# A two-layer transformer on one core: attention begins in another order, sums of x and y are spread, second bank for the slots' outputs, other order of gathers, fewer sort products

## The reference, cut to what matters

```python
x = x + L0_xattn(ctx_1024, layernorm(x))   # state-space scan over 256 steps, gated by silu(z); z = layernorm(x)
x = x + L0_ffn(layernorm(x))               # 32 experts of width 96, all computed, 8 of them weighted
x = x + L1_xattn(layernorm(x), ctx_1024)   # q = x @ Wq, 16 heads, 8 kv heads, softmax, @ Wo
x = x + L1_ffn(layernorm(x))               # shared part + top 2 of 16 experts

# L1_ffn
shared = swiglu(x, wg_s, wu_s, wd_s) * 0.1
affinity = sigmoid(einsum('bsh,eh->bse', x, centroids))
_, top_idx = top_k(affinity + gate_bias, 2)
weights = top_aff / (top_aff.sum(-1, keepdims=True) + 1e-9)
for e in range(16):
    routed = routed + mask[..., e:e + 1] * swiglu(x, wg[e], wu[e], wd[e])
return shared + routed
```

## Time and profile before

| | us |
|---|---|
| median of 3 runs | 692.14 (691.43 to 693.7) |
| the profiled execution, its own time | 690.36 |
| its span | 688.6 |
| TensorE busy | 625.7 (91%) |
| VectorE busy | 488.7 (71%) |
| ScalarE busy | 385.8 (56%) |
| GpSimd busy | 275.2 (40%) |

### The profile page before, as it was taken

How to read it: one execution, slowest core, us unless ns; L and a number is a source line. 1 busy time by engine, 2 the same in 40 slices (tenths; PEclk the granted TensorE clock), 3 DMA queues, 4 the chain that set the end, 5 groups by cost and what they waited for, 6 DMA issues and landing times.

```text
span 688.6 us, 10769 instructions
## 1 busy us (share of the span) xinstructions
PE 625.7 (91%) x3640; PEld 511.1 (74%) x3640; DVE 488.7 (71%) x1034; ACT 385.8 (56%) x790; POOL 275.2 (40%) x280
## 2 busy tenths in 40 slices
PE   7657759999999999999979999999999999999894
PEld 2346535554677888888868999999899988778773
DVE  5999999999976565446456766668577865654365
ACT  4866667644146546445367777777876765423221
POOL 1356610002144444445444655655455861241204
PEclk9789999999999999999999999999999999999998
DMA  6677844665645354444229232242111221355524
GB/s 194 200 270 265 278 156 149 204 204 178 182 130 173 104 177 124 154 153 150 79 90 339 96 135 79 83 147 78 32 31 47 78 78 47 123 171 166 181 96 122
DMA packets 58134, 98.89 MB, mean 144 GB/s; under 512 B 7000, under 2 KB 26976, under 8 KB 58080
## 3 DMA queue, kind: packets, MB, share of 16 engines
q1 hardware_dynamic: 56544, 94.00, 43.0%
q0 software_dynamic: 1536, 4.20, 1.9%
HBM read 78.51 MB, written 19.66 MB: 143 GB/s over the span
## 4 chain that ended last, share of the span: by engine, by line
PE 58%; DVE 26%; issue 7%; ACT 6%; another core or an unknown queue 1%; POOL 1%; DMA 0%; DVEq 0%; SPq 0%; ACTq 0%; POOLq 0%
PE bank L97 15%; PE bank L98 14%; PE bank L99 14%; DVE state L1432 10%; PE bank L884 5%; DVE read_out L1442 4%; PE bank L822 3%; PE bank L905 2%; ACT probs L1262 2%; PE bank L873 2%; ACT bank L1015 1%; DVE u_sb L1358 1%; DVE x_tok L1456 1%; DVE bank L1697 1%
## 5 line engine op out<-in xcount | busy, mean ns | idle before, releaser
L1994 POOL TENSOR_TENSOR w_lo<-w_raw,w_hi 128x768 fp32r<-128x768 f32 (+1 forms) x70 | 112.5, 1609 | 171.7 <-ACT w_hi L979 169.4
L97 PE MATMUL bank<-xt_hi,w_hi 128*128 128x512 f32 x224 | 91.1, 406 | 1.3 <-DVE hidden_lo L1349 1.3
L98 PE MATMUL bank<-xt_lo,w_hi 128*128 128x512 f32 x224 | 88.7, 396 | 0.0
L99 PE MATMUL bank<-xt_hi,w_lo 128*128 128x512 f32 x224 | 88.5, 395 | 0.0
L979 ACT ACTIVATE w_hi<-w_raw 128x768 fp32r<-128x768 f32 (+1 forms) x70 | 52.1, 745 | 58.4 <-PE bank L99 46.4
L1262 ACT ACTIVATE probs<-scores,row_min 128x256 f32<-128x256 f32 x128 | 63.8, 501 | 18.7 <-DVE row_min L1825 18.5
L2101 POOL TENSOR_TENSOR probs<-probs,row_scale 128x512 f32<-128x512 f32 x64 | 66.6, 1040 | 5.0
L1825 DVE CUSTOM_DVE_ANT_0 scores<-bank,mask_bias 128x256 f32<-128x256 f32 x128 | 48.8, 419 | 18.7 <-PE bank L99 18.7
L979 ACT ACTIVATE probs_t_hi<-bank 128x512 fp32r<-128x512 f32 x64 | 38.2, 598 | 36.8 <-PE bank L822 36.1
L510 PEld LDWEIGHTS bank<-identity,read_out 128*128 128x128 f32 x272 | 34.4, 153 | 30.8 <-DVE read_out L1442 17.9
L1130 ACT ACTIVATE gated<-bank 128x512 f32<-128x512 f32 x52 | 31.1, 597 | 42.1 <-PE bank L604 26.9
(11 more groups left out here) (233 smaller groups left out, 1747.0 us busy)
## 6 DMA issues: line engine op xcount, KB each, us to landing
w_raw<-in_ffn_w SPq DMA_DIRECT2D x38, 384.0 KB, 3.5
b_rows<-bc_scratch SPq DMA_DIRECT2D x32, 256.0 KB, 4.9
c_rows<-bc_scratch SPq DMA_DIRECT2D x32, 256.0 KB, 4.0
w_raw<-fold_scratch SPq DMA_DIRECT2D x32, 256.0 KB, 2.9
experts<-in_ffn_w SPq DMA_DIRECT2D x16, 384.0 KB, 4.2
route_bc<-route_scratch SPq DMA_DIRECT2D x31, 192.0 KB, 3.4
slots_scratch<-nothing SPq DMA_DIRECT2D x2, 2944.0 KB, 13.2
slots_in<-slots_scratch SPq DMA_DIRECT2D x22, 256.0 KB
```

What stands on the lines that cost most here:

```text
L97: e.matmul(out, w_hi, m_hi, start=first, stop=False)
L98: e.matmul(out, w_hi, m_lo, start=False, stop=False)
L99: return e.matmul(out, w_lo, m_hi, start=False, stop=last)
L1994: e.tensor_tensor(lo[:, 0:n], w_raw[(p - WHOLE) % RAW][:, 0:n], hi[:, 0:n].bitcast(F32), ALU.subtract).then_inc(sem("w_lo"), 1)
```

## The change

Six edits, none of which adds or drops a result:

1. y's sums of the second half: the first batch's stay where they were, the second batch's and the variance move to the next FFN unit.
2. Attention's beginning. `project(0, 0)` stands before `down(U0 - 1)`; `scores(0)` and `scores(1)` come next, and only then `project(0, 1)` and `project(1, 0)`. ACT and DVE follow that order. The table of exponentials is loaded after the FFN's last silu. Weight pieces are split one unit later.
3. The steps of x for the second half move from units 2 to 7 to units 3 (both additions), 5 and 7 (sums), 9 (variance), 10 (POOL's power), 11 and 12 (normalising), 13 and 15 (transposes and their splits).
4. `sel_sums` holds running sums of `sel` over the chunks, made by DVE with a copy and three additions; `count_earlier` needs 3 products in place of 8.
5. `down_slots` uses bank 3 for the odd rounds 9 to 21, bank 2 for all others.
6. The lower slots (m = 1) are gathered and added first, and their gathers wait for all rounds of the half but the last; the higher slots' gathers wait for that one too.

```diff
+        def out_bank(r):
+            return 3 if r % 2 == 1 and 9 <= r <= ROUNDS - 2 else 2
...
-                for j in range(1, HC):
-                    e.matmul(ps[:, j * E1:HC * E1], every[:, :], flat[:, 0:(HC - j) * E1], start=False, stop=False)
-                for j in range(HC):
-                    last = e.matmul(ps[:, HC * E1:(HC + 1) * E1], every[:, :], sel[:, j, :], start=False,
-                                    stop=j == HC - 1)
-                last.then_inc(sem("places"), 1)
+                e.matmul(ps[:, E1:HC * E1], every[:, :], sel_sums[:, 0:HC - 1, :].rearrange("p j n -> p (j n)"),
+                         start=False, stop=False)
+                e.matmul(ps[:, HC * E1:(HC + 1) * E1], every[:, :], sel_sums[:, HC - 1, :],
+                         start=False, stop=True).then_inc(sem("places"), 1)
...
-            down(U0 - 1)
...
-            for q in range(GROUP):
-                project(0, q)
+            project(0, 0)
+            down(U0 - 1)
             for i in range(HEAD_UNITS + 4):
                 if i < HEAD_UNITS:
                     scores(i)
+                if i == 1:
+                    project(0, 1)
+                    project(1, 0)
...
-                if i < HEAD_UNITS and i % HB == 0:
+                if 0 < i < HEAD_UNITS and i % HB == 0:
                     project(i // (GROUP * HB) + 1, i // HB % GROUP)
-                if 6 <= i <= 7:
-                    transition(5, i - 1)
+                if i in (13, 15):
+                    transition(5, 5 + (i - 13) // 2)
...
+                if u == U0 - 1:
+                    e.preload_act_table_set("exp_and_others")
...
+                own.step(e.tensor_copy(sel_sums[:, 0, :], sel[:, 0, :]))
+                for j in range(1, HC):
+                    own.settle()
+                    last = e.tensor_tensor(sel_sums[:, j, :], sel_sums[:, j - 1, :], sel[:, j, :], ALU.add)
...
                 if n == DS + 1:
                     gate_y(1)
-                    add_y(1)
+                    add_y(1, range(1))
+                if n == DS + 2:
+                    add_y(1, range(1, HB))
...
-                for i in range(3):
-                    at.wait_ge(f"outs_stored{i}", 16 * (((h + 1) * PAIRS - i + 2) // 3))
                 at.wait_ge("routed", h * HC * TOP1)
-                for m in range(TOP1):
+                for m in (1, 0):
+                    for i in range(3):
+                        at.wait_ge(f"outs_stored{i}", 16 * (((h + 1) * PAIRS - m - i + 2) // 3))
```

More of the change, by code:

```diff
@@ L1283, in activate_slots @@
                              ACT.Silu).then_inc(sem("slots_silu"), 1)
-            for q in range(GROUP):
-                round_projected(0, q)
+            round_projected(0, 0)
             for i in range(HEAD_UNITS + 4):
@@ L1457, in add_to_x, with add_y @@
                 at.wait_ge(name, count)
-            def add_y(h):
-                for b in range(HB):
+            def add_y(h, batches=range(HB)):
+                for b in batches:
                     at.wait_ge("y_gated", 2 * h + b + 1)
@@ L1915, in route_first_half @@
                     find_weights(6, (i - 25,))
-            for q in range(GROUP):
-                rest_projected(0, q)
-            for i in range(HEAD_UNITS + 4):
+            rest_projected(0, 0)
+            mask_scores(0)
+            mask_scores(1)
+            invert_sum(0)
+            rest_projected(0, 1)
+            invert_sum(1)
+            for i in range(2, HEAD_UNITS + 4):
                 if i < HEAD_UNITS:
```

60 lines of the change are left out of this document (41 added, 19 removed).

## The result

| | before | after |
|---|---|---|
| median, 7 runs of each, us | 694.52 (691.43 to 694.95) | 687.03 (682.83 to 689.26) |
| the profiled execution, us | 690.36 | 687.4 |
| its span, us | 688.6 | 685.6 |

The ratio is 0.9898, with the interval 0.9868 to 0.9928. The forecast, 681.9, was 5.1 us too low, and the measured median lies just outside its range.

The account below looks back on a forecast made before the run. TensorE, busy 91% of the span, was taken as the bound. Gains 1.3 + 4.4 + 2.1 + 2.4 = 10.2 us from 690.36 gave 680.2, plus 1.8 for the median 681.9; 8-in-10 range 677.5 to 687.

Parts of the forecast that it names:

- The sum's start: Whole kernel: gains were subtracted from the profiled execution's 690.36 us, then 1.8 added for the median of the runs.
- I count nothing: First half's gathers: they begin one round sooner beside the same traffic, entered with no gain.
- If such stalls end with the last gather, as these two did, they move with it: Gathers: unexplained stalls, ACT's 5.3 us wait and a DVE addition 1.79 late, were taken to move with the last gather.
- y's sums, 1.3: End of the second scan: moving the second batch's sums removes TensorE's 1.31 us wait; 1.3 us won, bounds 0 to 1.3.
- Attention's beginning, 4.4: Attention's start: new product order (1.9 us) and spread steps of x win 4.4 us together, bounds -1.0 to 6.7.
- The half clock's 1.7: Attention's beginning: 3.4 us at half clock cost half of that, 1.7, counted as winnable beside 5.0 us idle.
- 0.45 + 1.4 + 0.45 = 2.3: Attention: 0.45 us waiting left at the start, 1.4 before unit 4's masking, 0.45 for x's steps in later units.
- Sort products, 2.1: Both sorts: three products instead of eight save TensorE 1.05 us each, 2.1 together; bounds -0.9 to 1.07 each.
- Second bank, 0.9: Last rounds: with bank 3, round 22's down products skip the wait for a copy and start 0.9 us sooner.
- Order of the gathers, 1.5: Kernel's end: lower slots gathered first, adding 1.5 us to the bank's 0.9; last gather and additions 2.4 sooner.
- the end does not follow the gathers: Rival: DVE slows descriptors or the stall ends at its own time; gathers' 1.5 us lost, 683.4 us; chance 0.12.
- the forecast's 10 us for gathers beside additions: Kernel's end: by the skill page alone, four gathers beside DVE additions would cost some 10 us more; not counted.

Follow-up runs that it names:

- y_later: Changed kernel with x's steps behind the second scan (second half of the first FFN) one FFN unit later; 685.21 us, ratio 0.9855 to before.
- best: Changed kernel with the first half's gathers one for each round and x's steps after the second scan one unit later; 677.38 us, ratio 0.9837 to before.
- best_b: The same kernel as best, run again on another chip; 677.39 us, ratio 0.9835 to before.
- before_again: The kernel before, run again with no edit; 696.85 us against 696.24, ratio 1.0011.
- late1: Changed kernel, its last half's gathers waiting for all rounds before the first, lower slots still first; 679.33 us, ratio 0.9880 to before.
- old_sort: Changed kernel with the eight sort products of before and no running sums on VectorE; 682.28 us, ratio 0.9909 to before.
- again: The changed kernel run again with no edit; 678.90 us, ratio 0.9853 to before.
- again_b: The changed kernel with no edit, run once more on another chip; 678.71 us, ratio 0.9862 to before.

## Why the prediction was wrong

Three steps failed: the base of the sum, 692.14, which is 694.52 in the longer series; the stalls of the earlier trace rows, which were entered without a term and took 2.4 us from the profiled pair; and y's 1.3, which measured 0. Only the third is a wrong mechanism of the edits themselves.

- **The sum's start.** "The profiled execution took 690.36 ... the median of the runs is 1.8 above that execution". Three runs gave the median 692.14; seven gave 694.52. The profiled execution was one of the few with the FFN's products 4 us early, and the 1.8 us added for the median didn't cover that. The earlier trace rows began at 215 us, and the first 200 were not asked what of their time was owed to the granted clock. Of the 5.1 us, 2.4 lie between the two medians of before (694.52 against 692.14). That the clock makes those 2.4 isn't shown: the runs behind the two medians have no trace.
- **"I count nothing"** for the first half's gathers, and "If such stalls end with the last gather, as these two did, they move with it" for the stalls of the earlier trace rows. They are no fixed price. Rounds 12 to 16 take 13.0 us without a stall, 15.75 in before's trace, 18.1 to 19.2 in five others. I saw a wait of 5.3 us without a cause in the very stretch, and entered it in the sum with its size of one execution. It took 2.4 of the profiled pair's gain, by luck of the pair: on B the stretch is longer in before. That it accounts for the other 2.7 us in the medians of the first comparison (7.5 against 10.2) is therefore not shown: of those fourteen runs only one has a trace. This part of the miss stays open.
- **y's sums, 1.3.** Measured 0. "x_shift is only needed a unit after that" was the wrong step: x's transposes and the route's products stand at fixed places of the following FFN units, and there TensorE now waits 1.14 us for the 1.31 that went. With those moved too (y_later, best, best_b) the stretch is 1.5 us shorter than in before. This is the one mechanism that the forecast had wrong in the kernel itself.
- **Attention's beginning, 4.4.** Measured 5.3 to 5.5. The order's part was right (1.8 for 1.9). The price in the steady units can't be told from the products that moved there: units 8 to 16 take 1.91 us more (28.12 for 26.21), and TensorE is 2.03 us less busy in units 0 to 8 (24.73 against 26.76 in before_again). The half clock's 1.7 was mis-sized as time (0.2), but without it TensorE would have idled 1.2 more in the same place, so the 6.7 that could be won were about right (6.52 in before_again). The mis-sized step is what was left of it: 0.45 + 1.4 + 0.45 = 2.3 forecast, 1.74 of idle time measured over the whole stretch, with 0.46 and 1.01 for its two largest waits. That makes 6.52 - 1.74 = 4.8 us less idle time against before_again, and TensorE's busy time is another 0.5 us lower (64.96 for 65.48), 5.3 in all.
- **Sort products, 2.1.** Measured 1.12 and 0.84.
- **Second bank, 0.9,** measured 0.8. **Order of the gathers, 1.5,** measured 1.86 by having the lower slots' gathers wait as before (the order itself was not undone), while in the first pair the end gained 1.42. The step "the last four additions, which begin 3.2 us behind it" failed: they begin 3.7 to 4.3 us behind it, since VectorE's other additions now end last. The forecast had looked for a second limit only in TensorE's last product. The rival "the end does not follow the gathers" is refuted in its size, since the 1.5 were won, but a gather that started sooner still would win nothing. The Trainium skill's rule on descriptors (page SBUF — State Buffer, section "SBUF: two separate sides") was no matter: a last gather that ran beside the additions of gathered rows took 1.16 us in before, 1.09 in before_again, 0.95 and 1.09 in late1, 0.95 and 1.23 in old_sort, and all others 0.94 or 0.95. The page has its about 3.1 us for a DMA beside a `tensor_copy`; it names copy, cast and `tensor_scalar` as operations that can take the port, says that `tensor_tensor` has no such mode, and doesn't name the additions used here. So the forecast's 10 us for gathers beside additions do not follow from it.

Terms measured by undoing them: 5.3 + 0 + 2.0 + 0.8 + 1.9 = 10.0 us, against 10.2 forecast, and on chips without the stall the unedited kernel shows 9.6 (again) and 8.9 (again_b). So the mechanisms of attention, sorts, bank and gathers were right and y's was not. That the sum of the terms came out so near is in part luck: y's 1.3 too many stands against 0.9 too few in attention. And the sum was laid on a base that was neither typical in its clock nor free of a stall: before alone has medians of 687.64 to 689.85 us on the five chips without the stall and 696.24 on B.

## What to carry to other kernels

Before a sum is taken from one profiled execution, ask what in that execution could be luck: the stretches at the half clock, and waits whose releaser had long been done. Both belong in the range with their full size, even where the edit doesn't touch them. And a step that is moved later in a hand-written order is free only if the steps behind it, which keep their places, can also be late: read each of them off before the wait is counted as won. The same holds where a limit is lifted: here VectorE's own row ended last as soon as the gathers came sooner.

## What the runs showed of the hardware

- While GpSimd issues eight indirect DMAs, ScalarE can wait 4.7 to 6.7 us, and VectorE 1.7 to 3.3, for something that no engine is busy on ("remote" in the profile); that a semaphore arrives late is the likely reading. It was in all four traces of chip B and in both of the first comparison, and in none of the 14 of the other five chips; it costs 3 us in the scatter's burst (rounds 4 to 6: 11.9 to 12.5 against 9.1) and 3 to 6 in the gathers' (rounds 12 to 16: 15.75 to 19.2 against 13.0). Its cause stays open, and that the burst of DMAs is part of it too.
- The same program, in different executions, has TensorE's 1.2 GHz stretches in its first 125 us in different number (3.4 us or 10 to 17 us of them between 93 and 122), and with more of them the later units come about 4 us later (eight products took 5.22 us there for 3.60).
- A half clock where TensorE waits anyway costs little: 3.4 us of it in attention's beginning cost 0.2 us of time, and not half of 3.4 (one pair of executions).
